# Two destinations in one count cell: a graph-sum kernel counts pairs as int32 and splits them per block

## The reference

```python
def sage_conv(x, edge_index, W_l, b_l, W_r, n):
    src, dst = edge_index
    agg = segment_sum(x[src], dst, num_segments=n)
    return agg @ W_l.T + b_l + x @ W_r.T
h   = relu(sage_conv(x, ...))            # 32 -> 64, first segment sum
x   = layernorm(x + sage_conv(h, ...))   # 64 -> 32, second segment sum
# then graph attention on the same edges: scores, softmax by destination,
# a message softmax with edge_attr (200000 x 2 x 32), a third segment sum
out = layernorm(x + attention(x, edge_attr, ...))
```

## Time and profile before

| | us |
|---|---|
| median of three runs | 4038.03 |
| span of the profiled execution | 4039.9 |
| set-up, 0 to 75 | 75 |
| pass `sum_x`, 75 to 1032 | 957 |
| dense stage, 1032 to 1075 | 43 |
| pass `sum_y`, 1075 to 1776 | 701 |
| the rest (attention, last layernorm), 1776 to the end | 2264 |

### The profile page before, as it was taken

The page is one execution under the profiler, slowest core; times in us unless marked ns, Lnnn a source line. Parts: engine busy times, 40 slices in busy tenths (PEclk is TensorE's granted clock), DMA queues, the critical chain, the costliest instruction groups (busy, mean ns, idle before and its releaser), DMA issues. The chain is left out here.

```text
span 4039.9 us, 77882 instructions
## 1 busy us (share of the span) xinstructions
PE 2838.7 (70%) x25297; PEld 2329.2 (58%) x25297; DVE 2627.6 (65%) x7797; ACT 2694.4 (67%) x7435; POOL 2939.3 (73%) x2929
## 2 busy tenths in 40 slices
PE   4778887888677777775576666766666666667655
PEld 2555555666466666664465655656556666556644
DVE  8978776656243333354357777777777788777876
ACT  4979887888665566541067667776767776677745
POOL 4877777777577777745777777777777777777735
PEclk9989999999898988886557777677767777777767
DMA  3556565566688888843333333433333433333311
GB/s 86 209 181 245 215 246 215 215 223 238 237 310 289 292 301 292 285 166 95 66 85 90 82 77 89 90 91 82 84 78 87 91 87 85 77 87 87 89 30 41
DMA packets 301014, 607.50 MB, mean 150 GB/s; under 512 B 121338, under 2 KB 211892, under 8 KB 292697
## 3 DMA queue, kind: packets, MB, share of 16 engines
q1 hardware_dynamic: 207232, 517.61, 36.3%
q0 software_dynamic: 88192, 82.32, 12.2%
q10 hardware_dynamic: 5185, 2.56, 0.2%
HBM read 394.37 MB, written 207.85 MB: 149 GB/s over the span
## 5 line engine op out<-in xcount | busy, mean ns | idle before, releaser
L858 POOL DMA_INDIRECT gath<-x_parts,src_idx x652 | 729.8, 1119 | 235.2 <-issue 227.4
L1987 POOL DMA_INDIRECT scratch<-fs_scratch,src_idx x728 | 720.8, 990 | 221.9 <-issue 221.0
L914 ACT ACTIVATE scratch<-sum_x_ps_c 128x600 bf16<-128x600 f32 (+7 forms) x1003 | 769.9, 826 | 158.3 <-PE sum_x_ps_c L945 137.9
L858 POOL DMA_INDIRECT gath<-y_parts,src_idx x540 | 516.8, 957 | 169.3 <-issue 164.0
L945 PE MATMUL sum_x_ps_c<-e_tab,scratch 128*128 128x300 bf16 (+7 forms) x2006 | 485.3, 325 | 139.4 <-ACT scratch L914 75.4
L2115 ACT ACTIVATE scratch<-scratch,bias,weight 128x32 f32<-128x32 f32 x1360 | 483.9, 400 | 92.1 <-DVE bias L2185 92.1
L2029 PEld LDWEIGHTS ps_e<-fdw,scratch 128*128 128x128 f32 x3136 | 503.6, 243 | 23.7
L1016 DVE TENSOR_SCALAR e_tab<-scratch 128x1300 bf16<-128x1300 f16 (+13 forms) x1024 | 450.4, 451 | 73.9 <-PE sum_x_ps_c L945 54.7
L2029 PE MATMUL ps_e<-fdw,scratch 128*128 128x66 f32 x3136 | 486.4, 323 | 0.0
L2196 DVE SCALAR_TENSOR_TENSOR scratch<-ps_e,attn_sb 128x128 f32<-128x128 f32 x784 | 189.5, 284 | 418.2 <-PE ps_e L2029 417.3
L2095 ACT ACTIVATE scratch<-iota,dst_rel 128x128 f32<-128x128 f32 x824 | 251.2, 388 | 280.0 <-PE ps_m L2049 270.8
(11 more groups left out here) (354 smaller groups left out, 6913.9 us busy)
## 6 DMA issues: line engine op xcount, KB each, us to landing
count_scratch<-scratch SPq DMA_DIRECT2D x58, 3200.0 KB
scratch<-count_scratch SPq DMA_DIRECT2D x232, 800.0 KB
onehot<-rel_scratch SPq DMA_DIRECT2D x196, 256.0 KB
scratch<-in_edge_attr_2x SPq DMA_DIRECT2D x390, 128.0 KB
fdw<-fd_scratch SPq DMA_DIRECT2D x392, 33.0 KB
scratch<-fs_scratch,src_idx POOLq DMA_INDIRECT x728
gath<-x_parts,src_idx POOLq DMA_INDIRECT x652
gath<-y_parts,src_idx POOLq DMA_INDIRECT x540
```

The costliest lines, as they stand in the source:

```text
L858: pool.indirect_dma_start(out=rows_in(s, t), out_offset=None, in_=table_dram, in_offset=bass.IndirectOffsetOnAxis(ap=src_idx[:, g, k:k + 1 ...
L914: act.activation(to, ps_c[u % pairs][:, :, 0:q].rearrange("p h (d a) -> p h a d", d=d), ACT.Copy).then_inc(kept, 1)
L1987: pool.indirect_dma_start(out=rows_of(m)[:, t, :], out_offset=None, in_=fs_dram, in_offset=bass.IndirectOffsetOnAxis(ap=src_idx[:, g, k:k ...
```

## The change

A count cell now stands for two neighbouring destinations: an edge adds 1 to it if its destination offset is even and 65536 if it is odd. `cells` is half as wide, and DVE's compare multiplies by the edge's weight (`head_weight`, a second per-partition operand). `keep` copies PSUM into an int32 view of `counts`, in which each cell takes the room of two bf16 numbers, so that its low and high 16 bits lie where the two destinations' bf16 counts belong. When a block is whole, DVE turns all its 12,800 16-bit halves per partition into bf16 in place (`tensor_copy`, an int16 view to a bf16 view), and the product and the store wait for that (`apart`) where they waited for `kept`. `lows` is now built for four tiles at a time, in another place in memory.

`CLASSES` has 9 classes of even spans instead of 15. `sum_x` counts 1032 tiles (690 units, 74 blocks) and gathers 67 slots (532 gathers; before 652), stores only its first 48 blocks; `sum_y` reads 48, counts the other 42 blocks (348 tiles, 348 units: 180 of 2x350 columns, 112 of 2x400, 56 of 2x450) itself, and gathers 52 slots (412 gathers; before 540).

```diff
-CLASSES = ((2, 64, 64), (3, 84, 42), (4, 64, 32), (5, 72, 24), (6, 63, 21), (7, 72, 18), (8, 80, 16), (9, 84, 14),
-           (10, 96, 12), (11, 66, 11), (12, 50, 10), (13, 99, 9), (14, 18, 9), (14, 48, 8), (15, 64, 8))
-FIRST_TILES = 912
+CLASSES = ((2, 64, 64), (4, 160, 32), (6, 160, 20), (8, 144, 16), (10, 156, 12), (12, 120, 10), (14, 180, 9),
+           (16, 112, 8), (18, 56, 7))
+FIRST_TILES = 1032
+STORED = 48
+PAIR = 65536.0
...
+                link(dve.tensor_scalar(odd[:, 0:T1], offset[:, 0:T1], 1, None, ALU.bitwise_and))
+                link(dve.tensor_scalar(head_weight[:, 0:T1], odd[:, 0:T1], PAIR - 1.0, 1.0, ALU.mult, ALU.add))
+                link(dve.tensor_scalar(half[:, 0:T1], offset[:, 0:T1], 1, None, ALU.logical_shift_right))
...
-                    for b in range(len(plan.blocks) if store else 0):
-                        sp.wait_ge(kept, kept_before(b))
+                    for b in range(STORED if store else 0):
+                        sp.wait_ge(apart, b + 1)
                         sp.dma_start(count_dram[b, :, :], counts[:, b % 2, :, :].rearrange("p a q -> p (a q)"))\
...
                         act.wait_ge(counted, u + 1)
                         if unit["pieces"] == 1:
-                            to = counts[:, w, :, unit["column"]:unit["column"] + 2 * d]\
+                            to = in_pairs[:, w, :, unit["column"]:unit["column"] + 2 * d]\
...
                             if i == 0:
                                 if b >= read:
-                                    pe.wait_ge(kept, kept_before(b))
+                                    pe.wait_ge(apart, b - read + 1)
...
+                    def make_lows(group):
+                        before = (group - RING + 1) * LOWS - 1
+                        if before >= plan.first_tile:
+                            dve.wait_ge(counted, counted_to(before))
+                        tiles = slice(group * LOWS, (group + 1) * LOWS)
+                        dve.tensor_tensor(lows[:, group % RING, :, :], wide(count_up[:, 0:P], 1, [P, LOWS, P]),
+                                          wide(head_low[:, tiles], 2, [P, LOWS, P]), ALU.is_equal)
...
                             d = dve.tensor_scalar(cells[:, n % RING, i * width:(i + 1) * width], count_up[:, 0:width],
-                                                  head_key[:, tile:tile + 1], None, ALU.is_equal)
...
+                                                  head_key[:, tile:tile + 1], head_weight[:, tile:tile + 1],
+                                                  ALU.is_equal, ALU.mult)
...
+                        for b, i, _ in plan.products.get(step, ()):
+                            if i == 0 and b >= read:
+                                dve.wait_ge(kept, kept_before(b))
+                                w = plan.buffer(b)
+                                dve.tensor_copy(counts[:, w, :, :], halves[:, w, :, :]).then_inc(apart, 1)
...
-        segment_sum_pass("sum_y", ys_dram, flat_rest, Plan(head, head.first_blocks, HB), False)
+        segment_sum_pass("sum_y", ys_dram, flat_rest, Plan(head, STORED, HB), False)
```

More of the change, by code:

```diff
@@ L19 @@
 I32 = mybir.dt.int32
+I16 = mybir.dt.int16
 BF16 = mybir.dt.bfloat16
@@ L50 @@
 NOWHERE = 1 << 20
[L54 to L56 removed]
+CLASSES = ((2, 64, 64), (4, 160, 32), (6, 160, 20), (8, 144, 16), (10, 156, 12), (12, 120, 10), (14, 180, 9),
[3 more added lines that the diff above has]
+PAIR = 65536.0
 HEAD_TILES = sum(tiles for _, tiles, _ in CLASSES)
[L58 removed]
+WIDEST = max(span for span, _, _ in CLASSES) // 2
+assert all(span % 2 == 0 for span, _, _ in CLASSES)
+CELLS = 1000
 ALL_HIGHS = 100
@@ L62 @@
 LEAD = 2
+LOWS = 4
 QUARTERS = 4
@@ L67, in pieces_of @@
 def pieces_of(span):
-    return next(n for n in (1, 2, 4) if span * ALL_HIGHS // n <= BANK)
+    return next(n for n in (1, 2, 4) if span // 2 * ALL_HIGHS // n <= BANK)
 def class_ranges():
@@ L101, in __init__ @@
                     item = len(self.items)
+                    self.item_of += [item] * step
                     banks = [(item, i, (i * pieces + piece) * size) for i in range(step) for piece in range(pieces)]
-                    self.items.append({"tiles": list(range(t, t + step)), "span": span, "first": len(self.units),
+                    self.items.append({"tiles": list(range(t, t + step)), "pairs": pairs, "first": len(self.units),
                                        "last": len(self.units) + len(banks) // 2 - 1})
                     for u in range(len(banks) // 2):
-                        self.units.append({"banks": banks[2 * u:2 * u + 2], "block": block, "span": span,
-                                           "column": (t - tile) * span, "size": size, "pieces": pieces,
+                        self.units.append({"banks": banks[2 * u:2 * u + 2], "block": block, "pairs": pairs,
+                                           "column": (t - tile) * pairs, "size": size, "pieces": pieces,
                                            "highs": slice(2 * u * ALL_HIGHS // pieces, (2 * u + 2) * ALL_HIGHS // pieces)})
@@ L122, in __init__ @@
         self.first_item = head.units[self.first_unit]["banks"][0][0]
+        self.first_tile = head.blocks[read]["tile"]
         self.end_unit = head.blocks[blocks - 1]["end"]
@@ L814, in segment_sum_pass @@
                 counts = scratch[:, 0:COUNTS].bitcast(BF16).rearrange("p (w a q) -> p w a q", w=2, a=NK)
-                ring = e_tab[:, :, :, :].rearrange("p g k h -> p (g k h)").bitcast(BF16)
-                cells = ring[:, 0:RING * WIDEST * NK].rearrange("p (i q) -> p i q", i=RING)
+                halves = scratch[:, 0:COUNTS].bitcast(I16).rearrange("p (w a q) -> p w a q", w=2, a=NK)
+                in_pairs = scratch[:, 0:COUNTS].bitcast(I32).rearrange("p (w a q) -> p w a q", w=2, a=NK)
+                ring = flat_e.bitcast(BF16)
+                assert all(len(item['tiles']) * item['pairs'] * NK <= CELLS for item in head.items)
+                cells = ring[:, 0:RING * CELLS].rearrange("p (i q) -> p i q", i=RING)
                 ps_c = [ctx.enter_context(nc.psum_tensor(f"{tag}_ps_c{i}", [P, 2, 512], F32)) for i in range(3)]
@@ L869, in _ @@
                     if store:
-                        sp.wait_ge(stored[0], (len(plan.blocks) + 1) // 2 * 16)
+                        sp.wait_ge(stored[0], (STORED + 1) // 2 * 16)
                     for b in range(read):
@@ L897, in keep @@
                         unit = head.units[plan.first_unit + u]
-                        b, q, d = unit["block"], unit["size"], unit["span"]
+                        b, q, d = unit["block"], unit["size"], unit["pairs"]
                         w = plan.buffer(b)
@@ L944, in count @@
                             for h, (item, i, at) in enumerate(unit["banks"]):
-                                m = pe.matmul(ps_c[u % pairs][:, h, 0:q], lows[:, item % RING, i, :],
+                                tile = head.items[item]["tiles"][i]
+                                m = pe.matmul(ps_c[u % pairs][:, h, 0:q], lows[:, tile // LOWS % RING, tile % LOWS, :],
                                               cells[:, item % RING, at:at + q], start=True, stop=True)
```

76 lines of the change are left out of this document (44 added, 32 removed).

## The result

The changed kernel takes 4588.1 us (median of 4 runs, 4584.4 to 4589.9) against 4039.1 us beside it: ratio 1.1355 [1.1338, 1.1371], 549 us slower. The forecast was 4280 (+241), its range ended at 4520. The direction was right, the size was not. The profiled execution spans 4586.3 us.

What follows compares the result with a forecast made beforehand. Prediction: POOL's gathers bound both passes of the kernel before. 4040 + 73 (`sum_x`) + 169 (`sum_y`) + 0 (set-up) = 4,282, so 4,280 us; range 4,080 to 4,520, the forecast's own 4,150 to 4,420.

Steps and rivals of the forecast that it cites:

- The conversion: DVE turning a block's 12,800 16-bit halves into bf16 was to take 3.8 us, at the pace of the cells.
- `sum_x`, POOL: In `sum_x`, 532 gathers at 1.25 us plus 235 us of holds by conversions, 28 behind: 1,028 us.
- the strict rule: Fast two-port DVE instructions shut GpSimd out throughout; POOL's 500 and DVE's 550 us would add, `sum_x` ending near 1,080.
- `sum_x`, PE's chain: In `sum_x`, PE's 616 us of work plus 340 idle before products; with early blocks about 1,010 us, 6 more at the end.
- `sum_x`, the two chains together: In `sum_x`, PE's and POOL's chains were called equally long, waiting for each other: 1,030 us, +73.
- `sum_y`: The pass was to take 870 us, +169: keeps 290, lends 168, conversions with products and hops 362, first counts 38, ends 12.
- the ring: In `sum_y`, once per own block, keep waits for the previous product, product for conversion, conversion for last keep: 858 us.
- The bound of 950: Upper bound for `sum_y`, 950 us: PE at a clock of 0.89 throughout and a later DVE.
- Slow int32 writes: Rival: in `sum_y`, ACT's int32 keeps as slow as its scattered fp32 row, 230 us more; 4,510 us in all, chance 0.06.
- Gathers saved win: Rival: fewer gathers shorten both passes, `sum_x` to 785 and `sum_y` to 539 us; 3,706 in all, chance 0.10 with half-way forms.
- POOL sets both passes: Claim on the kernel before: POOL's gathers, 928 us in `sum_x` and 681 in `sum_y`, determine the passes of 957 and 701.
- rival 3: ACT writing int32 keeps slowly in `sum_y`, 230 us on top: 4,510 us in all, chance 0.06.

Runs made afterwards that it cites:

- the run whose pass took 1027: Changed kernel with quartered conversions, later `sum_x` product and window, ScalarE making `sum_x`'s one-hots, `sum_y` lends ahead, 54 blocks stored: 4115.2 us, 1.0163 against the kernel before.

## Why the prediction was right or wrong

- **The conversion**, forecast 3.8 us: 3.50. Right. It is 0.27 ns an element, the pace of 16-bit cells. The Trainium skill's "Vector Engine (DVE) Microarchitecture Reference", section 5.1, gives the four-a-cycle mode to `tensor_scalar`, copies and casts alike when all operands are two bytes wide and in SBUF; the trace agrees, for int16 too.
- **`sum_x`, POOL**, forecast 1,028: the term was right, and wasn't last. 100 + 235 us of holds over 532 gathers of 944 ns give 1574 ns a gather; it was 1590, and the parts were 110 and 233 us. Where the other waits were taken away, the pass came to 1027 to 1066. By the strict rule weighed there (the Trainium skill, "SBUF — State Buffer", "Who interferes with whom") the gathers' own 502 us and VectorE's two-port instructions would add up. If cells and conversions are these, as the prediction's 550 us had it, they are 625 us in the run whose pass took 1027. The sum would be 1,127, so then the rule does not hold in full for these gathers. (A gather that is held counts as busy, so busy times side by side decide nothing here.)
- **`sum_x`, PE's chain**, forecast 616 + 340, with early blocks 1,010: **this step failed.** The waits for conversions were about right (313). PE's own 616 us were taken at a clock of 1.00, read where PE never stopped, and the 340 us of waits were then added as if they left that clock alone. PE's work took 816 us; with the waits filled, about 680 (904.67 less 4,736 dummies at 3.04/64 us = 225). The pass paid 112 for it. (The Trainium skill, "TensorE: Matmul & The Clock Gate", section "HAM oscillation — how this bites in real kernels", tells of a kernel whose TensorE falls back to 1.2 GHz at every wait for its next operands and starts each group of matmuls slowly; the trace agrees for the 66 and 23 products that began at the lower clock, with 0.50 and 0.99 above, and the prediction had not weighed it.) The other 108 us, of 220: with the waits filled PE's work is still 64 above 616, and the waits for cells and keeps are 127 in place of some 54, less the 27 by which the waits for conversions came out shorter. Of the waits for cells, 57 of 90 us lie before 400 us, in the early blocks, where the prediction had them. What makes the 64 us was not tested. That a conversion stops VectorE, whose lead is two units, and so stops PE a second time, shows in the versions with a later product (248 us); in the changed kernel no wait for cells ends within 6 us behind a conversion.
- **`sum_x`, the two chains together**: "equally long" was wrong. PE's work and its waits for conversions alone are 1129 us, POOL's gathers with their issue 1035.
- **`sum_y`**, forecast 870: the ring was right, with ScalarE's 455 us of work (forecast 458) and, between one block's last keep and the next one's first, a wait of 10.6 us on average (forecast 3.8 + 4.41 + 0.4 + 0.9 = 9.5). Of the 78 us too little, 54 are the clock, by the run with dummies: the product was priced at 4.41 us and took 6.22 on average. ScalarE's shorter waits for counts between its keeps, some 40 us, had been put at nothing. That PE's work "hides beside ACT's" was too much said: with 168 us of lends off the line only 49 came back. The bound of 950 is near what came, partly by luck: it had a clock of 0.89 throughout, but also a later DVE, which no run shows, and not these waits.
- **Slow int32 writes** (a rival): no. 348 keeps took 279 us, forecast 290.
- **Gathers saved win** (a rival): 120 fewer would have been worth 171 us in `sum_x` if POOL had set the pass; already with a conversion of 0.57 us `sum_x` is 956. The reason lies in part in the kernel before: followed back through its `sum_x`, the chain lies on ScalarE for 245 us, on PE for 236 and on POOL for 217. "POOL sets both passes" was right for `sum_y` (505 of 701 on POOL) and too much said for `sum_x`.
- **The range**: its upper end was rival 3 alone. The low clock was priced in `sum_y`'s bounds and not in `sum_x`'s. At the 0.80 that was measured, 616 us are 770, PE's chain 1,164, the forecast some 4,420 and its upper end some 4,650.

## What to carry to other kernels

A wait that a change puts into PE's list can have two prices: its length, and the work at the lower clock behind it; here a wait of some 4 us cost 1.3 to 1.5 us more each. Price PE's work at the clock it will have with the new waits, and test it with dummy matmuls in the wait: if the time falls, the clock was costing time. If it doesn't, look for what else is last, and remember that the dummies are work too. In this kernel an instruction of several us on VectorE, which runs two units ahead of PE, was not hidden by moving one consumer after the other; pieces of 0.99 us, about as long as a unit, each signalled and stored by itself, did better.

## What the runs showed of the hardware

In `sum_x` of the changed kernel, where PE stood still for 4.2 us on average before each product, 362 of its 816 us of work ran at a granted clock of 0.50 (1.2 GHz). 64 matmuls that nobody reads, 3.04 us of work in each wait, took that to 82 of 905 us and made the program 165 us shorter. The lower clock did not always begin with the work behind the wait: of the 116 products 27 began at 2.4 GHz, most of them behind waits of 3.5 to 4.0 us, and one of these fell to 1.2 GHz after 1.04 us.

A gather takes 0.94 us by itself. Many that began up to 1.1 us before a conversion were held until 0.12 us after its end (3.65 us beside 3.50 above). Of the 15 that began under one in `sum_x`, 13 ended 0.81 to 0.82 us after it, like this one, which ends at 1133.71, 0.82 us behind the conversion:

```profile
1129.40 3.49 DVE L1079 CAST scratch<-scratch 128x12800 bf16<-128x12800 int16 x1 [0.42 <-ACT scratch L942]
1129.73 3.98 POOL L885 DMA_INDIRECT gath<-x_parts,src_idx  x1 [0.30 <-issue]
```

The conversions took 3.47 to 3.68 us, whichever began first. Conversions of 0.99 us in place of 3.50 left the sum of gather time nearly the same in `sum_x` (842 and 823 us in two versions, before 846), but not in `sum_y` (504 to 444).
